# A graph layer of edges in 52 blocks: one-hot products in f32, one for three, and a last block with its index loads moved up

## The reference

```python
def _L0_gnn_ref(Z, U, Dmat, head_w, edge_index):
    src, dst = (edge_index[0], edge_index[1])
    ZU = jnp.einsum('nd,kdr->knr', Z, U)
    zs = ZU[:, src, :]
    zd = ZU[:, dst, :]
    logits = (zs * zd).sum(-1) / scale
    seg_max = jax.vmap(lambda l: jax.ops.segment_max(l, dst, num_segments=N))(logits)
    exp_l = jnp.exp(logits - seg_max[:, dst])
    seg_sum = jax.vmap(lambda e: jax.ops.segment_sum(e, dst, num_segments=N))(exp_l)
    alpha = exp_l / (seg_sum[:, dst] + 1e-16)
    weighted = alpha[..., None] * zs
    agg = jax.vmap(lambda w_: jax.ops.segment_sum(w_, dst, num_segments=N))(weighted)
    ...
x = _layernorm(x + _L0_gnn_ref(x, ...), axis=-1)
x = _layernorm(x + _L1_gnn_ref(x, ...), axis=-1)
```

## Time and profile before

| | |
|---|---|
| median of the runs | 3771.14 us |
| all runs | 3765.44, 3793.86, 3771.14 us |
| the profiled execution | 3755.32 us |
| its span in the profile | 3753.5 us |
| mean granted clock of TensorE over the span | 0.572 of full speed |
| PE, DVE, POOL, ACT busy | 52%, 51%, 46%, 31% |
| the loop, from the first L922 to the last | 178.7 to 3265.3 us, 52 blocks |

### The profile page before, as it was taken

How to read it: one execution, slowest core, us unless ns; L and a number is a source line. 1 busy time by engine, 2 the same in 40 slices (tenths; PEclk the granted TensorE clock), 3 DMA queues, 4 the chain that set the end, 5 groups by cost and what they waited for, 6 DMA issues and landing times. The chain is left out here.

```text
span 3753.5 us, 61674 instructions
## 1 busy us (share of the span) xinstructions
PE 1961.4 (52%) x15249; PEld 1492.6 (40%) x15250; DVE 1919.1 (51%) x5861; ACT 1169.7 (31%) x3041; POOL 1721.7 (46%) x1833
## 2 busy tenths in 40 slices
PE   7344545454555445445445455354444554594776
PEld 7233434333343333333334334243333333453665
DVE  6344545445555445545455455455445544682566
ACT  2012222323323232323223232223232323353557
POOL 3544454444444444444444444544544444224662
PEclk8555555555555555555555555555555555597877
DMA  6211211121221212211112112121211121293343
GB/s 208 52 37 38 48 42 43 39 46 41 48 47 43 44 40 45 47 40 44 42 38 46 42 41 47 41 48 41 47 38 44 40 47 38 65 314 115 120 139 98
DMA packets 406592, 232.96 MB, mean 62 GB/s; under 512 B 284096, under 2 KB 371434, under 8 KB 406506
## 3 DMA queue, kind: packets, MB, share of 16 engines
q1 hardware_dynamic: 346666, 154.11, 15.0%
q0 software_dynamic: 59840, 77.87, 9.7%
HBM read 134.80 MB, written 42.55 MB: 47 GB/s over the span
## 5 line engine op out<-in xcount | busy, mean ns | idle before, releaser
L549 POOL DMA_INDIRECT arena<-z_table,sslot x1563 | 1487.8, 952 | 1702.9 <-SPq L400 1191.5
L1303 PE MATMUL bank<-arena 128*128 x4992 | 609.5, 228 | 564.2 <-issue 474.7
L1538 ACT ACTIVATE arena<-bank 128x272 f32<-128x272 f32 x416 | 268.4, 662 | 1614.6 <-remote 983.0
L1303 PEld LDWEIGHTS bank<-arena 128*128 128x128 bf16 x4992 | 469.3, 107 | 708.9 <-issue 616.4
L850 DVE TENSOR_TENSOR xin<-arena,bank 128x512 f32<-128x512 f32 x208 | 142.9, 687 | 1034.3 <-remote 697.3
L1515 ACT ACTIVATE acc<-xTb 128x68 f32 x1600 | 386.6, 312 | 350.1 <-issue 339.6
L1320 PE MATMUL bank<-xto,arena 128*128 128x68 bf16 x3328 | 330.7, 246 | 218.9 <-issue 218.8
L1320 PE MATMUL bank<-arena 128*128 128x68 bf16 x1664 | 300.3, 244 | 211.1 <-issue 135.0
L1320 PEld LDWEIGHTS bank<-xto,arena 128*128 128x128 bf16 x3328 | 284.7, 132 | 242.1 <-issue 241.7
L1291 PE MATMUL bank<-ident_b,arena 128*128 128x128 bf16 x1664 | 211.0, 306 | 317.9 <-remote 132.1
L841 DVE TENSOR_SCALAR arena<-iota_b,didx 128x128 bf16<-128x128 bf16 x1664 | 302.0, 264 | 40.8 <-issue 34.2
(11 more groups left out here) (250 smaller groups left out, 2493.2 us busy)
## 6 DMA issues: line engine op xcount, KB each, us to landing
arena<-arena SPq DMA_DIRECT2D x1660, 32.0 KB
arena<-z_table,sslot POOLq DMA_INDIRECT x1563
dspace<-in_xT SPq DMA_DIRECT2D x49, 256.0 KB
xmz_table<-agn SPq DMA_DIRECT2D x49, 256.0 KB
x_table<-arena SPq DMA_DIRECT2D x14, 896.0 KB, 4.9
arena<-in_x SPq DMA_DIRECT2D x13, 896.0 KB, 11.0
out<-arena SPq DMA_DIRECT2D x12, 896.0 KB
xin<-in_xT SPq DMA_DIRECT2D x8, 896.0 KB
```

The source lines that it names most:

```text
L549: pool.indirect_dma_start(ring[:, e % RING, :], None, z_table, bass.IndirectOffsetOnAxis(ap=sslot[:, e:e + 1], axis=0)).then_inc(tiles_in[ ...
L1303: last = T.matmul(zd_ps[g % 2][:, u * KR:(u + 1) * KR], onehotT[:, g * G + u, :], z3[:, bass.ds(tiles[u], 1), s, :].rearrange("p a c -> p ...
L1538: A.activation(sums[:, :, 1 + q * Q:1 + (q + 1) * Q].rearrange("p c j -> p j c"), sum_ps[q % 2][:, 0:Q * AW].rearrange("p (j c) -> p j c", ...
```

## The change

- **Products in f32.** z3 is gone, and zf stays where z3 was. One-hots are written in f32 (half 0 in the arena, half 1 in the buffers xto and xin), the transposes read the top bf16 half of each, and the transposed one-hots are f32. A step of the expansion is one f32 matmul instead of three in bf16, and so is a step of the sums. leave_rest and leave_low are gone from DVE, and the splitting of zf in the prologue (28 operations on DVE, 4 on ACT).
- **Sums between the expansions.** add_up takes quarters 0 to 3, then 4 and 5, then 6 and 7, instead of 0 and 1, 2 and 3, 4 to 7.
- **Last block.** ACT, DVE and POOL load their indices ahead of the scan, in one list each; the 4 padding steps aren't stored (28 stores, in 7 rounds of 4); the scan of the block before runs in four pairs of its 12 parts between the scans of the maxima, and the last four parts behind x_ready (before: four times three, all ahead of it). SP's loads of x at the end change their order.

```diff
 def top(ap):
-    return ap.bitcast(BF16).rearrange("p j (c two) -> p j c two", two=2)[:, :, :, 1]
+    return ap.bitcast(BF16).rearrange("p (c two) -> p c two", two=2)[:, :, 1]
...
-        z3 = part((NT + 1) * ZP * KR // 2).bitcast(BF16).rearrange("p (t s c) -> p t s c", s=ZP, c=KR)
+        zf = part((NT + 1) * KR).rearrange("p (t c) -> p t c", c=KR)
...
-        onehot = part(B * P).bitcast(BF16).rearrange("p (h j n) -> p h j n", h=2, j=B)
-        onehotT = part(B * P // 2).bitcast(BF16).rearrange("p (j e) -> p j e", j=B)
+        onehot0 = part(B * P)
+        onehotT = part(B * P).rearrange("p (j e) -> p j e", j=B)
...
+        onehot1 = (xto_flat[:, 0:(B - G) * P], xin_flat[:, 0:G * P])
...
+            tiles = last_tiles(mybir.EngineType.Pool, 3)
+            pool.wait_ge(scan_done, NB)
+            pool.wait_ge(state_stored, B * (NB - 1))
+            for n in range(STORES):
+                if n >= 1:
+                    pool.wait_ge(last_stored[1], n)
...
-            z_remainder(0, 0)
-            z_remainder(1, 0)
...
-                    last = V.tensor_scalar(onehot[:, h, j, :], iota_b[:, :], didx[:, h, j:j + 1], None, ALU.is_equal)
+                    last = V.tensor_scalar(hot(h, j), iota_b[:, :], didx[:, h, j:j + 1], None, ALU.is_equal)
...
-                    n = len(SCAN_PARTS) // NG
-                    part_done = scan_parts(state_a, SCAN_PARTS[g * n:(g + 1) * n])
-                    if g == NG - 1:
-                        part_done.then_inc(scan_done, 1)
-                        end_scan(b - 1, state_a)
+                    scan_parts(state_a, SCAN_PARTS[2 * g:2 * g + 2])
...
+                if not more:
+                    scan_parts(state_a, SCAN_PARTS[2 * NG:]).then_inc(scan_done, 1)
+                    end_scan(b - 1, state_a)
...
-                weigh(0)
-                weigh(1)
-                if not first:
-                    dve.wait_ge(sums_ps, (B // Q) * b)
-                leave_rest(0)
-                weigh(2)
...
+                for g in range(NG):
+                    weigh(g)
...
-                    last = T.transpose(tr_ps[g % 2][:, u * P:(u + 1) * P], onehot[:, h, g * G + u, :], ident_b[:, :])
+                    last = T.transpose(tr_ps[g % 2][:, u * P:(u + 1) * P], top(hot(h, g * G + u)), ident_b[:, :])
...
-                    for s in range(ZP):
-                        last = T.matmul(zd_ps[g % 2][:, u * KR:(u + 1) * KR], onehotT[:, g * G + u, :],
-                                        z3[:, bass.ds(tiles[u], 1), s, :].rearrange("p a c -> p (a c)"), start=(s == 0), stop=(s == ZP - 1))
+                    last = T.matmul(zd_ps[g % 2][:, u * KR:(u + 1) * KR], onehotT[:, g * G + u, :],
+                                    zf[:, bass.ds(tiles[u], 1), :].rearrange("p a c -> p (a c)"), start=True, stop=True)
...
-                        pe.wait_ge(parts_ready, NG * b + q // 2 + 1)
-                    js = slice(q * Q, (q + 1) * Q)
-                    parts = (top(zs[:, h, js, :]), top(rest[:, js, :]), low[:, js, :])
+                        pe.wait_ge(weighted, NG * b + q // 2 + 1)
                     for u in range(q * Q, (q + 1) * Q):
-                        for s in range(ZP):
-                            last = T.matmul(sum_ps[q % 2][:, (u % Q) * AW:(u % Q + 1) * AW], onehot[:, h, u, :], parts[s][:, u % Q, :],
-                                            start=(s == 0), stop=(s == ZP - 1))
+                        last = T.matmul(sum_ps[q % 2][:, (u % Q) * AW:(u % Q + 1) * AW], hot(h, u), zs[:, h, u, :], start=True, stop=True)
...
-                add_up(b, h, 0, 2)
+                add_up(b, h, 0, 4)
                 if more:
                     expand(b + 1, 2)
-                add_up(b, h, 2, 4)
+                add_up(b, h, 4, 6)
                 if more:
                     expand(b + 1, 3)
-                add_up(b, h, 4, 8)
+                add_up(b, h, 6, 8)
```

More of the change, by code:

```diff
@@ L65 @@
 NSPARE = 4
-ZP = 3
 AW = KR + K
@@ L483, in _ @@
             sp.wait_ge(logits_ready, NB)
-            for g in range(4):
+            sp.wait_ge(sums_ps, (B // Q) * (NB - 1))
+            for g in (0, 1, 2, *range(6, 11)):
                 load_rows(g)
@@ L490, in _ @@
                 load_xmz(g)
-            for g in range(6, 8):
+            for g in range(3, 6):
                 load_rows(g)
@@ L672, in table_out_of_psum @@
                 last.then_inc(tab_read, 1)
-            def z_remainder(s, half):
-                dve.wait_ge(z_parts, 2 * half + s + 1)
-                if s == 0:
-                    dve.wait_ge(z_out[half], 16 * T7)
-                for t in range(half * NT // 2, (half + 1) * NT // 2, T7):
-                    part = slice(t, t + T7)
-                    to = zf[:, part, :] if s == 0 else z3[:, part, ZP - 1, :]
-                    last = V.tensor_tensor(to, zf[:, part, :], z3[:, part, s, :], ALU.subtract)
-                last.then_inc(z_rest, 1)
             dve.wait_ge(src_in, 16)
@@ L1017, in _ @@
             period(NB - 1, 1, NB // 2, more=False)
+            tiles = [last_tiles(mybir.EngineType.DVE, lane) for lane in (1, 2)]
             begin_scan(NB - 1)
```

144 lines of the change are left out of this document (46 added, 98 removed).

## The result

The changed kernel takes 3728.77 us (median of four runs, 3704.04 to 3786.55) against 3768.29 us: a ratio of 0.9868, 95% interval 0.9826 to 0.9911. It is 1.3% faster where 3.4% slower was forecast.

A forecast was written before the change was run, and what follows sets the result against it. PE's products, in the live time between slow stretches while POOL gathers, were taken to bound the kernel. Loop +140, prologue -3, last block +2 gave +139 on 3755.3; forecast 3900 us, range 3610 to 4070.

The forecast's parts named there:

- The rate of the f32 products: Expansion and sums on PE: 0.42 us a product at 1.2 GHz, 0.22 at 2.4 GHz, 64 products a block.
- What they cost the kernel: Loop: later L922 delays x_ready by 0.8 of 3.5 us, so 2.8 us a block, times 50 blocks, +140 us.
- The clock: PE in the loop: each live stretch begins at 1.2 GHz and the clock rises late in it, if at all.
- Where the products land: 56 products ahead of L1340: 13 to 24 left for the slow stretch's end, L922 2.5 to 7 us later.
- DVE at nothing: Dropping L980 and L985, 5.7 us a block on DVE, was taken to gain nothing, at most 0.5 us a block.
- The order at nothing: Four quarters of sums ahead of expansion 2 instead of two: no cost beyond the 56 products counted.
- One-hots at nothing: F32 one-hots on DVE within the scans: taken at 0, at most +0.7 us a block (35 us in all).
- The ends: Prologue -3 us (0 to -5) and last block +2 us (between -4 and +5).
- The sum itself: 140 - 3 + 2 = +139 on the profiled 3755.3 gives 3894; median 15.8 above the profiled run; forecast 3900.
- D: Rival: slow stretches cost per instruction, fewer instructions gain at most 1.3 us a block, 3705 us; chance 0.08.

The follow-up runs named there:

- b_nol_ord: Kernel before without DVE's eight operations and with the changed kernel's order of sums, first kind of chip: 0.9754 of the kernel before.
- a_both3: Changed kernel with expansion and sums in three bf16 matmuls a step, top halves alone, one register instruction a step: 3582.08 us, 0.9511 of the kernel before.
- a_again: Changed kernel run again unaltered, on a chip of the second kind: 2592.73 us against 2532.94 for the kernel before, 1.0215.
- a_dbl: Changed kernel with every f32 product of the sums issued twice, first kind of chip: 4304.14 us, 1.1407 of the kernel before.
- b_noleave_s: Kernel before without DVE's eight operations of 128x544, sums taking the top half three times, first kind of chip: 0.9842 of the kernel before.
- b_order_s: Kernel before with the changed kernel's order of sums, first kind of chip: 3700.09 us, 0.9839 of the kernel before.
- b_order: Kernel before with the changed kernel's order of sums, on a chip of the second kind: 0.9977 of the kernel before.

## Why the prediction was wrong

**The rate of the f32 products: right. What they cost the kernel: wrong.** 16 products in 7.04 us are 0.44 each, forecast 0.42. The forecast made 2.8 us a block of it, +140, and +139 with the ends. Measured, the f32 products, the f32 one-hots and the ends cost 43 us together (b_nol_ord to the change), 0.8 us a block. The split among them isn't measured. That a_both3 lies 134 us below the change looks like the forecast's 140, but is chance: it is measured against another bf16 form.

**The clock: wrong.** I took it to rise in the loop from the earlier trace rows. In the window above it stayed at 0.50 through 25.5 us of unbroken products. In a_again, on a chip of the second kind, both cases stand next to each other: windows, and PE's timeline:

```profile
1000.00:1016.00 16.00, 16.00 (x76) 16.00 (x77) 2.38 (x4) 3.53 (x6) 11.04 (x12) 0.50 0.23 52
1036.00:1048.00 12.00, 12.00 (x107) 11.80 (x105) 7.53 (x15) 4.00 (x6) 6.85 (x8) 1.00 0.33 85
```

```profile
1004.48 3.61 PE L1258 MATMUL bank<-arena 128*128 x16
...
1030.45 2.02 PE L1285 MATMUL bank<-mz,dspace 128*128 128x256 f32 x4
...
1033.13 1.70 PE L1285 MATMUL bank<-mz,dspace 128*128 128x256 f32 x4
...
1042.11 1.99 PE L1258 MATMUL bank<-arena 128*128 x16
```

16 us of unbroken products leave the clock at 0.50; it comes up around the dense part's L1285, and the same products then run at 1.00 through the 12 us of the window (16 records in 1.99 us, not 3.61). In the profile of after it came up around L1285 in the same way in one block, and was 1.00 from 1538 to 1548, but was down at 0.54 from 1548 to 1550 while products ran without a break, some 2 us after a pause of 1.11 us. In the prologue of before the rise that I laid to L1201 follows another form, which I had overlooked:

```profile
39.56 2.47 PE L1218 MATMUL bank<-ident,xto 128*128 128x128 f32 x13
...
42.10 1.08 PE L1201 MATMUL bank<-ur,xin 128*128 128x64 f32 x8
```

13 f32 transposes (L1218) lie right where the clock rose, at 41 to 42. What brings it up is not settled by these traces: in the loop of before it was also at 0.50 from 222 to 229, under bf16 expansion and sums, and at 1.00 from 229.2 to 232.4. The Trainium skill (TensorE: Matmul & The Clock Gate, Part 1) says that sustained activity releases the clock. This case doesn't bear that out for the f32 products: with PE busy for 100% of 25.5 us the granted clock stayed at 0.50.

**Where the products land: wrong.** The step was "the slow stretch does 8 records, which is 4 products", with 13 to 24 products left for its end and L922 2.5 to 7 us later. The trace of before had shown what bf16 matmuls, bound by issue, do there. f32 products were done at full rate for the first 6 us in which DVE and ACT had stopped (2297 to 2303), and none was left at its end: L906 came 2.1 us earlier in this block, and 1.5 in the median of the usual blocks. That products cost time nevertheless (b_nol_ord against the change, a_dbl) is measured; where in the loop they do isn't taken apart.

**DVE at nothing: wrong, and with the order what turned the sign.** "I take nothing, at most 0.5 us a block": it is 1.6% in the kernel before, 60 us, 1.2 us a block. The earlier trace rows count how long PE's sums waited for L985, and that is short; but the operations stand on DVE in the first slow stretch, ahead of fac and the head products, and those free the banks of the next expansions. I looked at one consumer. The first half of this is in the traces: without the operations (b_noleave_s) the first head product starts 12.2 us behind x_ready in the median of the blocks, with them (before) 15.2. How the rest of it reaches x_ready is argued, for the last head product comes at 41.6 us instead of 42.0. In the usual block after, L838 starts 11.3 us behind x_ready (2285.28), and L850 in the block of before 15.6 (timeline of DVE):

```profile
1538.99 0.21 DVE L1003 TENSOR_SCALAR fac<-bank,first_col 128x4 f32<-128x4 f32 x1
1539.41 0.69 DVE L850 TENSOR_TENSOR xin<-arena,bank 128x512 f32<-128x512 f32 x1 [0.21 <-DVE fac L1003]
```

**The order at nothing: wrong.** "L1340 stands behind all of them as before" is true and beside the point: what counts is how much stands behind expansion 3 when the long slow stretch begins. It is worth 1.6% (b_order_s), or 61 us, alone, and together with the DVE operations 2.5%, 93 us (b_nol_ord).

**One-hots at nothing: too low where it can be seen.** The scans are 1.1 us a block longer on chips without slow stretches, above the 0.7 that I gave as the most; what it costs is open. **The ends: not to be told.** The last block was +2.5 us (forecast +2), the prologue -7.9 (forecast -3, bound -5), in one pair of executions, and executions differ by more than that in the prologue.

**The sum itself** had a slip: 3894 and the 15.8 of the median make 3910, not 3900.

In sum on the first kind of chip: DVE's operations and the order -93 us, forecast 0; all the rest of the change +43, forecast +139; together -50, which is the 1.3%. Both errors were needed for the wrong sign: with the forecast's +139 and the measured -93 the change would still have cost 46 us, and with DVE and the order at nothing 43. Of the rivals the measured 3729 is nearest to D (3705). D said that fewer instructions have to crawl through the slow stretches, DVE's eight and PE's register instructions among them. It is not refuted: DVE's eight are worth 60 us, and a_both3, with 32 register instructions a block as the change has, is faster than b_nol_ord with 96. But on chips without slow stretches DVE's eight are worth 1.0% too, and no run has the register instructions alone.

## What to carry to other kernels

Costing several edits at nothing is a claim for each of them: where one term of the sum rests on a good row and the others on "hidden", the others together can be larger. An experiment that takes a part back has to bring the old form back whole, register instructions and all: count the instructions of its line in both traces before the difference is called the price of the part. Where engines stop for stretches at a time, look not only at who waits for an operation on the mean, but also at what it pushes behind the next stop. And before a rate or a clock is taken from a stretch of the trace, look at every line that runs in it, not only at the one that interests.

## What the runs showed of the hardware

- The same program takes 3768 us on some chips and 2533 on others (two of the six that ran the experiments). On the first kind PE, DVE, ACT and SP nearly stop while POOL issues indirect DMAs 1.25 us apart (before: 8 matmuls in 17 us, nothing on DVE and ACT, three transfers issued by SP); with 1.55 us from one to the next they don't. On the second kind they don't at 1.25 us either.
- 25.5 us of unbroken f32 products of 128x64 and 128x68 ran at 0.50 of the clock (after). In a_again the same products ran at 1.00 for 12 us, after a rise around L1285.
- 24 bf16 expansion matmuls took 1.2 us with one register instruction for three of them (a_both3), and 3.1 to 3.2 with one for each (before, b_order).
- A fill of 0.33 us on POOL behind each gather moved the gathers from 1.25 to 1.55 us apart.
